# A Mamba block and a routed feed-forward on one core: the order of VectorE's scans, who forms the products with C, and the chain behind the loop

## The reference, cut to what matters

```
x = x + attn(cond(x))            # x: 2 batches x 1024 tokens x 256
x = x + ffn(cond2(x))
cond:  a 256x256 matrix per batch (base + low-rank terms weighted by cond_8)
attn:  a two-way Mamba block, inner width 512, 16 states:
       dA_t = exp(dt_t * A[n]);  dBx_t = (dt_t * x_t) * B_t[n]
       h_t  = dA_t * h_{t-1} + dBx_t          # over the 1024 tokens
       y_t  = sum_n h_t[n] * C_t[n] + x_t * D # then gated, and projected to 256
       once forwards and once on the flipped sequence
cond2: a 256x256 matrix per batch, and a bias
ffn:   router (8 experts, the best 2 of a token), out = X + sum over its experts of
       W2[e] @ (silu(W1[e] xs) * (W3[e] xs)), xs = the token times its softmax weight
```

## Time and profile before

| | |
|---|---|
| median of 3 runs | 1400.84 us (1396.48 to 1401.32) |
| the profiled execution | 1394.14 us, its span 1392.3 us |
| granted TensorE clock, mean | 0.978 |
| busy over the span | PE 93%, DVE 68%, ACT 52%, POOL 69% |
| first `du` to the last own product (the loop) | 37.8 to 918.2 us |
| behind the loop, to the first tile's W1 | 918.2 to 959.5 us |
| experts and the end | 959.5 to 1392.3 us |

### The profile page before, as it was taken

One profiled execution on the slowest core, in us unless ns is written; L12 is line 12 of the kernel. 1 busy time (PEld: TensorE's weight loads), 2 busy tenths in 40 slices (PEclk: granted clock), 3 DMA queues, 4 the chain that ended last, 5 costly groups with the idle time before them and its releaser, 6 DMA issues. The chain is left out here.

```text
span 1392.3 us, 16616 instructions
## 1 busy us (share of the span) xinstructions
PE 1294.3 (93%) x5296; PEld 778.4 (56%) x5296; DVE 940.7 (68%) x1140; ACT 723.1 (52%) x1296; POOL 964.5 (69%) x511
## 2 busy tenths in 40 slices
PE   8999989999999989899797878899999999999997
PEld 3443333344333333333343333457999999999996
DVE  3999999999999999999999999963111111111110
ACT  4888776778785677676767564413111111111111
POOL 1999999999999999999999999832222222222211
PEclk9999999999999999999999999999999999999999
DMA  5555465555556464555456554508988888888982
GB/s 209 181 167 176 160 166 166 166 167 173 173 171 181 149 184 153 165 168 176 159 181 186 185 174 146 189 8 310 351 312 315 319 316 324 301 323 316 324 306 46
DMA packets 105497, 290.40 MB, mean 209 GB/s; under 512 B 9649, under 2 KB 19506, under 8 KB 89922
## 3 DMA queue, kind: packets, MB, share of 16 engines
q1 hardware_dynamic: 95762, 271.24, 56.3%
q0 software_dynamic: 9648, 18.09, 6.5%
HBM read 271.47 MB, written 9.96 MB: 202 GB/s over the span
## 5 line engine op out<-in xcount | busy, mean ns | idle before, releaser
L451 PE MATMUL ps_y<-arena,ident 128*128 128x512 f32 x1020 | 497.3, 619 | 55.0 <-POOL arena L1204 54.7
L1204 POOL TENSOR_TENSOR arena<-arena 128x1024 f32<-128x1024 f32 x192 | 457.4, 2404 | 18.9 <-DVE arena L946 15.3
L451 PEld LDWEIGHTS ps_y<-arena,ident 128*128 128x128 f32 x1020 | 190.9, 195 | 322.9 <-issue 214.0
L1188 POOL TENSOR_TENSOR arena<-arena 128x1024 f32<-128x1024 f32 x127 | 303.9, 2393 | 6.0 <-issue 4.3
L737 ACT ACTIVATE ps_de<-arena,An 128x512 f32<-128x512 f32 x256 | 176.2, 688 | 225.2 <-DVE arena L943 224.3
L1257 POOL DMA_INDIRECT out_x<-arena x39 | 61.8, 1584 | 319.1 <-ACT arena L881 301.9
L927 DVE TENSOR_TENSOR ps_u<-ps_du,arena 128x512 f32<-128x512 f32 x256 | 178.6, 698 | 23.9 <-DVE arena L957 8.6
L1155 DVE TENSOR_TENSOR arena<-ps_du,arena 128x512 f32<-128x512 f32 x39 | 27.0, 691 | 232.8 <-PE ps_du L617 232.8
L737 ACT ACTIVATE arena<-arena,An 128x512 f32<-128x512 f32 x256 | 181.0, 707 | 0.0
L943 DVE TENSOR_TENSOR_SCAN arena<-ps_de,hlast,arena 128x512 f32<-128x512 f32 x128 | 163.0, 1274 | 1.0 <-ACT arena L737 1.0
L943 DVE TENSOR_TENSOR_SCAN arena<-ps_de,arena 128x512 f32<-128x512 f32 x128 | 155.3, 1214 | 3.7 <-ACT arena L737 3.7
(11 more groups left out here) (225 smaller groups left out, 1484.2 us busy)
## 6 DMA issues: line engine op xcount, KB each, us to landing
arena<-bc_scratch SPq DMA_DIRECT2D x256, 512.0 KB, 4.6
arena<-in_W SPq DMA_DIRECT2D x117, 1024.0 KB, 8.2
arena<-arena POOLq DMA_DIRECT2D x15, 512.0 KB, 5.0
arena<-in_xT SPq DMA_DIRECT2D x2, 1024.0 KB, 6.1
arena<-in_w2c SPq DMA_DIRECT2D x1, 2048.0 KB, 8.6
arena<-in_xT SPq DMA_DIRECT2D x4, 512.0 KB, 6.1
X_scratch<-stg SPq DMA_DIRECT2D x12, 128.0 KB, 4.8
out_x<-stg SPq DMA_DIRECT2D x12, 128.0 KB, 5.1
```

The lines of the kernel that those rows point to most:

```text
L451: t = e.matmul(Y[j][:, :], ident[:, :], hc[:, i % NP, j, :], start=False, stop=(n == 15))
L1188: e.tensor_tensor(uA[:, turn % 2, :, :], duA.rearrange("p (o t) -> p o t", o=1).to_broadcast([128, 2, TH]), ring[:, turn % NR, 0, :, :], A ...
L1204: e.tensor_tensor(hc[:, i % NP, :, :], hh[:, i % NH, :, :], c, ALU.mult).then_inc(gp_hc, 1)
```

## The change

1. `scans` is cut into `scan_a` (second block) and `scan_b` (first block), and the order of a unit on VectorE becomes `du`, `scan_a`, `u`, `scan_b`, own product.
2. `OWN` gets nine units in 32 for eight.
3. `xT2` runs k outside, c inside, and waits for the first half of X only before its first products; `warm(2, 2)` ahead of the counts is taken out; `warm(6, 5)` behind the lists becomes `warm(3, 5)`.
4. `lx` gets a place of its own, and `hidden` loses its wait for the stores from it.
5. GpSimd adds the residual to `lx` behind its first three fetches; SyncE stores those sums behind the second tile's weights, not ahead of the wait for the first fetch.

```diff
-OWN = (3, 7, 11, 15, 19, 23, 27, 31)
+OWN = (3, 7, 10, 14, 17, 21, 24, 28, 31)
...
-        lx = hT.rearrange("p a k t -> p (a k t)").rearrange("p (i c) -> p i c", i=4)
...
+        lx = af.view(4, 2 * C)
...
-            for k in range(2):
-                is_free(("o", 1, 0, k))
             for h2 in range(2):
-                for c in range(2):
-                    p = place["xT2", h2, c][0]
-                    for k in range(2):
+                for k in range(2):
+                    is_free(("o", 1, 0, k))
+                    for c in range(2):
+                        p = place["xT2", h2, c][0]
                         t = e.matmul(PS[p][:, 0:C], wbot[:, 1, k, c * 128:c * 128 + 128],
                                      X[1][:, k, h2 * C:h2 * C + C], start=(k == 0), stop=(k == 1))
-                    t.then_inc(full[p], 1)
+                        if k == 1:
+                            t.then_inc(full[p], 1)
...
-            warm(2, 2)
...
-            warm(6, 5)
+            warm(3, 5)
...
-            def scans(i):
+            def scan_a(i):
...
+
+            def scan_b(i):
+                q, th, pr, n = unit(i)
                 e.wait_ge(dv_u, i + 1)
...
+                scan_a(i)
                 u(i)
                 if i == 0:
                     second_weights(0)
-                scans(i)
+                scan_b(i)
                 if own(i):
                     own_product(i)
...
-                elif c == 0:
-                    for k in (2 * i, 2 * i + 1):
-                        e.wait_ge(l_lx[k], 16)
-                        e.wait_ge(l_st[2 + k], 16)
...
-            for i in range(4):
-                is_read(e, ("x2", 1, i))
-                x2, xt = lx[:, i, 0:C], lx[:, i, C:2 * C]
-                e.tensor_tensor(xt, xt, x2, ALU.add).then_inc(gp_sB, 1)
...
             for i in range(3):
                 fetch(i)
+            for i in range(4):
+                is_read(e, ("x2", 1, i))
+                x2, xt = lx[:, i, 0:C], lx[:, i, C:2 * C]
+                e.tensor_tensor(xt, xt, x2, ALU.add).then_inc(gp_sB, 1)
...
             load_2(0, at_0)
+            e.wait_ge(l_xi[0], 16)
+            load_13(1, at_1)
+            load_2(1, at_1)
             for i in range(4):
                 e.wait_ge(gp_sB, i + 1)
                 e.dma_start(out[T + i * 128:T + i * 128 + 128, :], lx[:, i, C:2 * C]).then_inc(l_st[2 + i], 16)
-            e.wait_ge(l_xi[0], 16)
-            load_13(1, at_1)
-            load_2(1, at_1)
             load_13(2, at_2)
```

## The result

The changed kernel takes 1407.12 us (median of 20 runs, 1396.91 to 1412.79) against 1398.47 for the kernel before in the same session (20 runs, 1394.97 to 1401.60): ratio 1.0059, 95% interval 1.0048 to 1.0071. It is slower by just over the 0.5% that counts, where "no change" had been forecast at 0.67. The time lies inside the range; the direction was missed.

The account below looks back on a forecast made before the run. VectorE was taken to set the loop's pace, GpSimd some 3% behind, then a serial chain and fixed experts. Loop -0.6 and chain -2.4 gave -3.0 us: 1391 on the profiled 1394.1, 1397.8 against the median; range 1388 to 1408.

Parts of the forecast that it names:

- part (b) of the chain: Behind the loop: without `warm(2, 2)` the counts start 1.2 us earlier; first `last_x2` products at half speed cost +0.6.
- (a): Behind the loop: `xT2` no longer idles 0.88 us for the second half of X, -0.86 us.
- a clock dip: Rival: the tail gives nothing, by a clock dip in the first tiles or the loads; 1400 us, chance 0.04.
- VectorE's own sum: Loop: units -16.0, `du` +2.7, small work +8.5, start and end +0.9, together -3.9 us.
- ScalarE: Loop: later copy of dt makes scans wait, +4.2, and `keep_last` +1.3; together +5.5 us, bounds 0 to 14.7.
- Buffer waits: Loop: VectorE's waits for TensorE to free the product buffer, 4.2 us, shrink as GpSimd is relieved, -1.0 us.
- the rival in which it sets the pace: Rival: GpSimd bounds the loop, all of its -8.6 us comes through; 1390 us, chance 0.17.
- The loop's total: Loop: VectorE -3.9, ScalarE +5.5, GpSimd and the rest -2.2, together -0.6 us.
- The Trainium skill's rule on semaphores: Rival on VectorE's order: semaphores cost nothing extra, so the order wins nothing; +7 to +9 us, 1409, chance 0.02.
- (c): Behind the lists: shorter `warm(6, 5)` alone gives nothing; W3 of tile 1 lands sooner as two fetches leave its way, -1.0 us.
- (d): Behind the loop: residual sums move into GpSimd's idle time and `hidden` loses waits already over; 0 us.
- slower by ScalarE's bursts: Rival in the loop: late decays bound to ScalarE's queue cost 14.7, not 5.5; +6.2 or +9 us, chance 0.12.

Follow-up runs that it names:

- 1.0060 to 1.0001: Changed kernel with `u` ahead of `scan_a` in every 16th unit: 1.0060 (1406.21 us); the same with `warm(2, 2)` put back: 1.0001 (1397.59 us).
- the kernel with one product: Changed kernel with `warm(1, 2)`, one dummy product, put ahead of the counts: ratio 1.0044 (1.0026 to 1.0062), 1405.00 us.
- the one execution caught above 1403 us: A single profiled execution of the changed kernel, nothing altered: 1403.55 us, with a loop of 890.3 us.
- the 1.0001 kernels: Old loop, changed chain, `warm(1, 2)`: 1397.20 us; changed kernel with `u` ahead of `scan_a` every 16th unit and `warm(2, 2)` back: 1397.59 us.

## Why the prediction was wrong, step by step

**The step that failed: `warm(2, 2)`, part (b) of the chain.** It was priced at -1.2 for the counts that start earlier and +0.6 for "the first of `last_x2` at half speed for a time". The -1.2 is what the products cost in the one trace that was read, in which they ran at half clock: the line alone takes the counts of the kernel before from +15.48 to +14.26. In the profiles in which the clock is full they cost nothing, since the old chain has its counts at +14.26 with them too. (With (a) the forecast was 2.06; 1.34 came in the first trace.) The half speed has another size: not one group but in the bad executions all four, 4 x 1.62 = 6.5 us, and the following 128x512 products. Taken alone on the kernel before, the line costs +7 us, where -0.6 was forecast. In the changed kernel, putting it back gives 2.7 to 6.3 us. The prediction had read from the earlier trace rows that the clock was already at half while the dummy products ran, and priced only the first group behind them at half. That the line keeps the half clock short is shown by taking it out (1.0051) and by putting it in (1.0060 to 1.0001, and 1.0059 to 1.0014). Among the rivals one did name a clock dip, at 0.04, with the tail giving nothing; it was priced at 2.4 us, not at 7.

From 936.05 to 949.96 us the four groups of `last_x2` kept TensorE busy at 0.50 without a rise, and behind the four 128x512 products it was at 0.98. The Trainium skill (TensorE: Matmul & The Clock Gate, Part 1: The HAM clock gate) says that sustained work brings the clock back up. These traces agree with it only in part. Such a return does come, in seven profiles during the very same counts and first groups, after 3.4 or 6.8 us. In three it did not come in 14 us of them, and in the loop it did not come in 13.7 us of mostly 128x512 products. So the shape of the products is not shown to be what decides.

What stays open: why the same missing line costs 7 us on the kernel before, 3 with the new loop and the old chain, and nothing with the old loop and the changed chain (0.9982 without, 0.9988 with). The long stretch was seen in three profiles. In none of the four profiled executions of the changed kernel itself was it caught; that its median of 1407 us comes from there is inferred from its mean clocks and from the kernel with one product, not shown. That inference is weak, since the loop's own time at half clock moves the mean clock too, and the one execution caught above 1403 us had its loss in the loop. Nor does the place of the fall decide by itself: counted from the loop's last product the clock fell at +12.86 on the kernel before without the line and at +12.85 with the old loop and the changed chain, and stayed down 20.5 and 3.4 us; in the changed kernel it fell at +13.58 with one product and at +13.51 and +13.54 with none, and stayed down 20.5, 3.4 and 3.4. What does decide is open.

**VectorE's own sum** was right: every distance within about 0.02 us (behind the last scan 1.14, in second halves 1.20, where 1.12 and 1.18 were taken). Its own work went from 866.2 to 860.3 us, -5.9, forecast -4.8 without the start.

**The start** was priced at 0.9 together with the end. The first `scan_a` alone waits 1.2 us for GpSimd, and in the other three profiles of this kernel two waits take 2.4.

**ScalarE** had the right mechanism and places (129: 0.88, 161: 0.86, 225: 0.74, for 0.9, 0.9 and 1.75), and too small a size: 13.1 us over the loop against 5.3, +7.8 for +5.5. Unit 17 waits 1.21 where 0.7 was forecast. The rest are waits that a gap of `u` had partly covered, such as units 135 (1.27), 206 (1.34) and 226 (1.35), which waited 0.55 to 0.65 before and which the early copy of dt leaves at 1.2 to 1.3: the argument that from scan_a to scan_a nothing moves did not hold for decays released behind a burst.

**Buffer waits** were forecast 1.0 shorter. They are 3.7 us in the changed kernel's first trace, 6.3, 9.9 and 7.2 in the others, 4.4 before; with the clock at half in the loop they grow by 4.2 us at one unit. That sign was wrong. The ring waits went as forecast (1.2 us). GpSimd's idle time rose to 31.3 us (forecast near 30), so the rival in which it sets the pace fell.

The loop's total was forecast at -0.6. It is +2.3 in the profiled pair, +5.2 on the mean of the profiled executions, +2.0 by the timed ratio of the loop alone (-0.1 to +4.1). This is the second term that failed. VectorE's saving came, and the waits for the other engines took it back. By timed ratios the parts are now +2.0 for the loop, +2.7 to +6.3 for the missing line and -1.7 for the rest of the chain, together +3.0 to +6.6, for +4.6 and +8.2 measured; the intervals of some 2 us each leave room for the difference.

**The Trainium skill's rule on semaphores** (VectorE: DVE Perf Modes, The DRAIN you can't avoid), by which the semaphore costs nothing and the order would win nothing, does not hold here: scan to `u` is 1.28 with the wait and 1.12 without, and VectorE's own work fell 11.5 us by the order. That the time did not fall has another cause, the waits for other engines.

**The rest of the chain.** (a) The idle 0.88 ahead of `xT2` is gone. (c) The second tile was forecast to start when its W3 lands, with 1.0 won by the fetches. Its loads are issued at 959.7 (+37.1; before +37.5) and it starts 10.3 us later (before 10.1), at +47.44 for +47.63, behind 1.50 us idle of TensorE. So the loads were not quicker and no 1.0 was won; that the idle time is the wait for W3 fits the forecast, but their landing isn't in the trace of after. (d) Nothing, as forecast. With the two dummy products in both, the changed chain ends at +470.1 and the old one at +471.1 to +471.4 where the clock stays full, and at +471.8 and +472.7 where it is at half for 3.4 us. So the other parts together win some 1.0 us, where 1.9 was forecast: (a) came whole (counts at +13.40 for +14.26) and (c) did not.

The rival "slower by ScalarE's bursts" named the right direction and the wrong place: waits for ScalarE stayed at 13 us, under the 17 from which it was to decide. Neither of the two signs came under which the forecast called itself wrong (a wider gap behind `u`, or GpSimd idle as before in a shorter loop): both looked at the loop, and none at the clock behind it. The best kernels by their medians are those that keep the old loop and take the changed chain: 0.9982 without the two products (0.9969 to 0.9996), 0.9988 with them (0.9974 to 1.0003). The intervals of these two and of the 1.0001 kernels overlap, so none is shown to be the best.

## What to carry to other kernels

Before taking out dummy products, ask what the granted clock is in the real work behind them, and price the whole of that work at half speed, not its first group. One execution can't show it, so look at the mean clocks of many, and at each stage's own clock before putting the mean down to one place. On an engine that sets the pace by 3%, work saved by a better order comes back as waits unless the releases of the other engines move with it: list what each moved instruction releases, and take the order back where a full queue hangs on it.

## What the runs showed of the hardware

Three things were not expected. TensorE, nearly always busy, stayed at the granted clock 0.50 for 20.5 us behind an idle gap of 1.8 us, or 0.8 with one product, in three profiles, and in the loop for 13.7 us in six, while in others it was back after 3.4 or 6.8 us of the same work. The same program spread over 16 us (1396.9 to 1412.8) with its mean clock (0.982 to 0.968), the kernel before over 6.6. And a wait of 4.2 to 4.9 us of VectorE's own product for TensorE came with 13.7 us at half clock in the middle of the loop, and never without.
